# Projections and the first feed-forward matrix as three float32r products of operands split in two, with weights loaded and split per layer, in a new order of work

## The reference, cut to what matters

```
def mha(qx, kx, wq, bq, wk, bk, wv, bv, wo, bo, mask, bias):
    q, k, v = (heads(t @ w + b) for t, w, b in ((qx, wq, bq), (kx, wk, bk), (kx, wv, bv)))
    a = softmax(mask(q @ k.T * scale + bias))
    return merge(a @ v) @ wo + bo
x = layernorm(x + mha(x, x, ...))        # attention 0, windowed
x = layernorm(x + mha(x, ctx, ...))      # attention 1
x = layernorm(x + gelu(x @ w1 + b1) @ w2 + b2)
...
```

## Time and profile before

| | |
|---|---|
| median of 3 runs | 3558.05 us (3555.76 to 3560.11) |
| profiled execution, from first to last instruction | 3565.0 us (no other time of it is given) |
| PE busy | 3446.8 us, 97% |
| DVE busy | 2572.8 us, 72% |
| ACT busy | 1935.0 us, 54% |
| POOL busy | 1143.4 us, 32% |
| granted TensorE clock, mean | 0.992 of 2.4 GHz |

### The profile page before, as it was taken

One profiled execution on the slowest core, in us unless ns is written; L12 is line 12 of the kernel. 1 busy time (PEld: TensorE's weight loads), 2 busy tenths in 40 slices (PEclk: granted clock), 3 DMA queues, 4 the chain that ended last, 5 costly groups with the idle time before them and its releaser, 6 DMA issues.

```text
span 3565.0 us, 53384 instructions
## 1 busy us (share of the span) xinstructions
PE 3446.8 (97%) x18672; PEld 1657.1 (46%) x18932; DVE 2572.8 (72%) x6523; ACT 1935.0 (54%) x2375; POOL 1143.4 (32%) x1049
## 2 busy tenths in 40 slices
PE   8899999999999999999999999999999999999998
PEld 5545544433454554443354455444335445445333
DVE  5766887756886588766778668777577956976667
ACT  2454565555555456555555545555564654655555
POOL 4322432222532242222253223222235322322222
PEclk9999999999999999999999999999999999999999
DMA  6311321223321231122332122112133312211211
GB/s 213 123 46 55 118 67 54 86 60 93 103 78 43 81 114 46 54 87 60 93 123 74 47 93 82 47 53 87 60 109 110 96 54 81 66 46 63 75 54 55
DMA packets 284317, 280.64 MB, mean 79 GB/s; under 512 B 49858, under 2 KB 275266, under 8 KB 280066
## 3 DMA queue, kind: packets, MB, share of 16 engines
q1 hardware_dynamic: 258324, 274.84, 24.0%
q10 hardware_dynamic: 25728, 2.36, 0.6%
HBM read 195.84 MB, written 81.26 MB: 78 GB/s over the span
## 4 chain that ended last, share of the span: by engine, by line
PE 83%; DVE 11%; issue 2%; ACT 2%; DMA 1%; SPq 1%; POOL 0%; another core or an unknown queue 0%; ACTq 0%; DVEq 0%
PE pv L718 14%; PE st L693 14%; PE mx L670 13%; PE mx L768 10%; PE mx L645 10%; PE st L731 9%; DVE row_max L911 5%; PE mx L742 4%; PE st L654 4%; PE mx L765 2%; PE st L778 2%; DVE mx L914 2%; ACT probs L829 1%; DVE turned L934 1%; DMA rows_of_max_dram<-max_rows 1%
## 5 line engine op out<-in xcount | busy, mean ns | idle before, releaser
L829 ACT ACTIVATE probs<-st 128x1024 f32<-128x1024 f32 (+1 forms) x1344 | 1266.6, 977 | 696.4 <-PE st L693 419.1
L911 DVE TENSOR_REDUCE row_max<-mx 128x1 bf16<-128x512 f32 x2048 | 1283.8, 684 | 216.3 <-PE mx L670 121.0
L1021 POOL TENSOR_TENSOR qm<-q_high,own_rows 128x512 bf16<-128x512 bf16 x768 | 797.3, 1044 | 1583.5 <-PE mx L670 1183.6
L670 PE MATMUL mx<-k_high,qm 128*128 128x512 bf16 (+4 forms) x2812 | 815.2, 342 | 44.7 <-DVE row_max L911 18.2
L693 PE MATMUL st<-q_packed,k_packed 97*128 97x512 bf16 (+2 forms) x3072 | 816.0, 346 | 27.3 <-DMA q_packed<-q_parts_dram 9.9
L718 PE MATMUL pv<-probs,va 128*32 128x512 f32 (+2 forms) x6144 | 701.8, 532 | 12.0 <-ACT probs L829 7.1
L670 PEld LDWEIGHTS mx<-k_high,qm 128*128 128x128 bf16 x3072 | 284.3, 98 | 604.0 <-DVE row_max L911 211.1
L914 DVE CUSTOM_DVE_ANT_0 mx<-mx,tab 128x192 f32<-128x192 f32 (+4 forms) x1024 | 400.9, 444 | 132.4 <-PE mx L670 118.7
L693 PEld LDWEIGHTS st<-q_packed,k_packed 97*128 97x128 bf16 (+1 forms) x3072 | 279.6, 98 | 435.0 <-ACT probs L829 149.8
L731 PE MATMUL st<-xT,w1s 128*128 128x512 f32 x768 | 342.9, 592 | 0.0
L957 DVE TENSOR_TENSOR y<-mx,row 128x256 f32<-128x256 f32 x224 | 94.8, 423 | 299.9 <-PE mx L768 297.2
(11 more groups left out here) (88 smaller groups left out, 3141.5 us busy)
## 6 DMA issues: line engine op xcount, KB each, us to landing
k_packed<-k_parts_dram SPq DMA_DIRECT2D x576, 128.0 KB, 2.7
q_packed<-q_parts_dram SPq DMA_DIRECT2D x576, 128.0 KB, 2.7
q_parts_dram<-q_low SPq DMA_DIRECT2D x96, 256.0 KB, 2.2
k_parts_dram<-k_low SPq DMA_DIRECT2D x96, 256.0 KB, 2.5
q_parts_dram<-q_high SPq DMA_DIRECT2D x48, 256.0 KB, 2.1
k_parts_dram<-k_high SPq DMA_DIRECT2D x48, 256.0 KB, 2.3
w1s<-w_dram SPq DMA_DIRECT2D x12, 1024.0 KB, 5.1
w2s<-w_dram SPq DMA_DIRECT2D x12, 1024.0 KB, 7.6
```

Of the source, the lines that this page charges most:

```text
L670: mm = pe.matmul(bank[:, 0:k1 - k0], qm[:, h % RING, i * P:(i + 1) * P], high["k"][s][:, t, k0:k1], start=True, stop=True)
L829: act.activation(dst[:, :, 0:w], held["scores", b, a, n, e][:, :, 0:w], ACT.Exp, scale=ATT_SCALE[a]) \
L911: ins = dve.tensor_reduce(top, scores, AX_X, ALU.max, negate=True)
L1021: pool.tensor_tensor(qm[:, h % RING], high["q"][s][:, h // HT], own_rows[:, h % HT:h % HT + 1].to_broadcast([P, TOK]), ALU.mult) \
```

## The change

The products of `project`, `project_v`, `hidden` and of the attentions' outputs are each written as three float32r matmuls. Both operands are cut in two: a high part, which ScalarE writes by a copy into a float32r tile, and a low part, which GpSimd computes as the original minus the high part. The product is then high x high + high x low + low x high. The second feed-forward matrix, scores, maxima, values, transpositions and folds stay as they were.

- Activations: new tiles `xh`/`xl` (state), `ch`/`cl` (context, and the input of a new pair) and `oh`/`ol` (attention output). A stage `low` cuts one half of an input, 128 x 2 x 256 or 128 x 512.
- Weights: `sq` now holds one layer's four squares in two parts. Stages `fetch` and `split` load one matrix (256 KB) into the single buffer `raw_w` and cut it, once for each pair of sequences; `fetch_w` and `split_w` do the same with quarters of `w1`. A fetch waits for GpSimd's part of the cut before. The folds' results go to DRAM and are fetched from there.
- Order: a sixth list of stages holds the weights' stages, and all strings of `MERGE` are new.

```
+def weight_stages(j):
+    b, a = LOOPS[j]
+    nb, na = (b // SLOTS * SLOTS + (SLOTS if a == 5 else 0), (a + 1) % 6)
+    if b % SLOTS:
+        yield from list(squares_of(nb, na, "qkv" if own(na) else "kvq"))[1:]
+    else:
+        yield from squares_of(b, a, "o")
+        if not j:
+            yield from w1_of(0, 0)
+        elif a in (2, 4, 5):
+            yield from w1_of(b + SLOTS * (a == 5), {2: 1, 4: 2, 5: 0}[a])
+        yield "fetch", nb, na, "q" if own(na) else "k"
...
 MERGE = {
...
-    "01": "011110111011101112301210111130111011101121122121011212103111011022111011211110011120010222222222"
-           "0002222020000222002002202220220200202220002222222",
...
+    "01": "101111102101104121101110101111130114212122432101110420110122101111022101431201201110112001221131"
+           "201222221022220220201230220202202202002022222020002022022020",
...
-        sq = sb("sq", [P, len(SQ), KT, D])
+        sq = sb("sq", [P, 4, 2, KT, D])
         w1s = sb("w1s", [P, KT, FF])
+        w1l = sb("w1l", [P, KT, FF])
+        raw_w = sb("raw_w", [P, KT, D])
...
+        def product(pe, bank, parts, start, stop):
+            for n, (stationary, moving) in enumerate(parts):
+                mm = pe.matmul(bank, stationary.bitcast(F32R), moving.bitcast(F32R), start=start and n == 0,
+                               stop=stop and n == len(parts) - 1)
+            return mm
...
+                elif kind == "fetch" and b < B:
+                    a, m = stage[2:]
+                    free_raw(stage)
+                    of = fold_dram[FOLDS.index(f"{m}{a}")] if f"{m}{a}" in FOLDS else square(f"{m}{a}")
+                    sp.dma_start(raw_w[:].rearrange("p k n -> p (k n)"), of).then_inc(raw_in, 16)
...
                     for t in range(KT):
                         bank = held["proj", b, a, m, t] = mx_bank()
-                        for j in range(KT):
-                            mm = pe.matmul(bank, sqw(f"{m}{a}")[:, j, t * P:(t + 1) * P], src[:, j, :],
-                                           start=(j == 0), stop=(j == KT - 1))
-                        mm.then_inc(*mx_filled.mark(("proj", b, a, m, t)))
+                        at = slice(t * P, (t + 1) * P)
+                        product(pe, bank, [(weight(m, w)[:, j, at], xs[:, j, :]) for j in range(KT) for w in range(2)], True, False)
+                        if t == 0:
+                            pe.wait_ge(*pool_step.past(("low", b, tag, 1)))
+                        product(pe, bank, [(weight(m, 0)[:, j, at], ls[:, j, :]) for j in range(KT)], False, True) \
+                            .then_inc(*mx_filled.mark(("proj", b, a, m, t)))
...
+                elif kind == "low":
+                    tag, p = stage[2:]
+                    highs, k, at = lows[low_place(b, tag)][0], *piece(tag, p)
+                    if p == 0:
+                        read = LAST_READ[b, tag]
+                        if read:
+                            act.wait_ge(*(mx_filled if read[0] == "mx" else st_filled).past(read[1]))
+                    act.wait_ge(*raw_made(b, tag, p))
+                    act.activation(highs[:, k, at].bitcast(F32R), raw(b, tag)[:, k, at], ACT.Identity) \
+                        .then_inc(*act_step.mark(("high", b, tag, p)))
...
+                elif kind == "split" and b < B:
+                    a, m = stage[2:]
+                    pool.wait_ge(*act_step.past(stage))
+                    pool.tensor_tensor(weight(m, 1).bitcast(F32R), raw_square(b, a, m), weight(m, 0), ALU.subtract) \
+                        .then_inc(*pool_step.mark(stage))
...
+                elif kind == "low":
+                    tag, p = stage[2:]
+                    (highs, rests), (k, at) = lows[low_place(b, tag)], piece(tag, p)
+                    pool.wait_ge(*act_step.past(("high", b, tag, p)))
+                    pool.tensor_tensor(rests[:, k, at].bitcast(F32R), raw(b, tag)[:, k, at], highs[:, k, at], ALU.subtract) \
+                        .then_inc(*pool_step.mark(stage))
```

405 lines of the change are left out of this document (280 added, 125 removed).

## The result

The changed kernel takes **3479.18 us** (median of four runs, 3478.05 to 3480.68), beside 3556.91 us (3555.37 to 3560.11) for the kernel before on the same chip: a ratio of 0.9778, 95% interval 0.9766 to 0.979. That is 78 us less. The forecast was 182 us less, 3375, and 3479 lies just above the upper end of the range, 3475.

A forecast was written before the change was run, and what follows sets the result against it. TensorE's queue was taken to set the time, with VectorE close behind in light stretches. From 3565 us, -192 for the pace, +7 and +2 for the ends gave 3382, scaled to a median of about 3375; range 3310 to 3475.

The forecast's parts named there:

- the two ends: Start and end of the kernel: 7 us later through the first projections, 2 us more at the last attention's output.
- I take the lower bound: 0.66 and 0.33 us per product. That saves ... 230 us.: Replaced products on TensorE: float32r at bf16's pace, 0.22 us for 512 columns and 0.11 for 256, saves 230 us of queue.
- I believe 60% of it there ... and 95% in the heavy ones.: Share of saved queue seen as time: 60% in light stretches (no feed-forward), 95% in heavy ones (the others); 192 us.
- Neither becomes the bound. The cover is what these engines have free.: 448 splits on ScalarE (65% of the span) and GpSimd (half) stay hidden in those engines' free time.
- The cover ahead of the first feed-forward: Element 0, last turn of x to first w1s product: 3.0 us of copies and splits hidden behind 4.9 + 0.9 us.
- Ends: +7 at the start.: First projection waits for low parts of wq and x; first complete product at about 17 us, three projections about 7 later.
- VectorE's share up to 76%: Sign of being right: VectorE's busy share of the span, 72% before, rises to 76%.
- light stretches that do not shrink: Sign of being wrong: stretches of a round without feed-forward do not get shorter at all.
- half pace: Rival, 10%: float32r streams at the pace of today's float32 halves, 495 us more, about 4050 us.
- the weight loads: Rival, 10%: three weight loads per product bind the 256-column products, 106 us of queue less, about 3465 us.
- The cover fails: Rival, 12%: splits late in ScalarE's or GpSimd's queue cost each of 48 stretches 2 us, about 3470 us.
- VectorE binds: Rival, 8%, said VectorE doesn't bind: maxima spread well, nearly all 230 us seen, about 3335 us or less.

The follow-up runs named there:

- run 2: Kernel before in its own order, each replaced product issued as three float32r matmuls of one constant rounded tile, no splits: 3408.57 us, ratio 0.9574.
- run 5: Changed kernel with GpSimd's 448 subtractions and ScalarE's 448 copies both cut to 16 columns: 3423.72 us, ratio 0.9616.
- run 4: Changed kernel with only GpSimd's 448 subtractions cut to 16 of 512 columns: 3422.1 us, ratio 0.9608.
- run 12: Changed kernel with each of the 448 subtractions issued as two of 256 columns, the 96 old 1024-column ones as two of 512: 3444.37 us, ratio 0.9682.
- run 7: Kernel before plus 432 GpSimd subtractions of 128x512 whose result nobody reads: 3585.24 us, ratio 1.0072.
- run 16: Kernel before in the new order, each replaced product as three float32r matmuls of constant tiles, no splits or fetches: 3412.52 us, ratio 0.9585.

## Why the prediction was wrong

From run 2 on there is a chain of medians: 3559 before, 3409 with the pace alone (-150), 3413 with the new order (+4), 3424 with fetches and short splits (+11), 3479 with GpSimd's full subtractions (+55 to 57). The forecast had -192 for the pace, nothing for the next three, and +9 for the two ends: 42 + 4 + 11 + 55 - 9 = 103 of the 104 us between 3375 and 3479.

- **"I take the lower bound: 0.66 and 0.33 us per product. That saves ... 230 us."** The mechanism was right, the size wrong. A float32r instruction goes at 0.233 us for 512 columns, a tenth slower than bf16's 0.213, and three of them make a product 0.70 us: 182 us of queue. This term alone is 48 us of queue, 40 of time. The 0.22 and 0.11 us were a lower bound taken as the value.
- **"I believe 60% of it there ... and 95% in the heavy ones."** Right. With 182 us a light stretch has 2.5 us to lose, a heavy one 5.1: 0.6 x 15.2 + 0.95 x 30.4 = 38 us a round, 152 in all, and run 2 gave 150. By kind it was 10.3 of 15.2 and 30.5 of 30.4 in the round looked at (four such rounds would be 163; the traced execution of before was 7 us longer than its median). This holds for the pace alone; in the changed kernel the held operations eat most of it.
- **"Neither becomes the bound. The cover is what these engines have free."** This step failed, and cost the most. The busy shares were right (ScalarE 62%, GpSimd 49%), ScalarE's copies are hidden (run 5), and TensorE hardly waits for a low part. But a GpSimd instruction isn't free for VectorE: while it runs, scale and `normal` stand still. The 448 subtractions cost 57 us (run 4), a term that the sum put at nothing. TensorE's waits for y and for row maxima, both made by VectorE, shrank by 39.5 us when they were cut. How much of the 57 goes this way is bounded and not fixed: halving the instructions' length, with more GpSimd work, gave 35 us back (run 12, in which the old 1024-column ones are halved too), and the same kind of instruction with no reader cost 26 in the old kernel (run 7). The rest may be low parts that come late or a shift of the whole schedule; no run separates it.
- **The cover ahead of the first feed-forward**, 4.9 + 0.9 us against 3.0: right. TensorE's idle time ahead of all 384 matmuls of x's low parts on w1 sums to 0.3 us.
- **Ends: +7 at the start.** The first projection starts at 17.31 us, as worked out ("about 17"), but the first attention ends at 98.4 us in place of 105.7. The relief for the resident squares' 2.5 MB, to which nothing was given back, is one candidate; no run separates it.
- **The order's own cost** was no term of the sum. It is 17 us in float32 and 4 at the new pace.
- **"VectorE's share up to 76%"** came out, 77%, by luck: the forecast got it from a shorter span, and the trace from 96 us more of VectorE's time in a longer one. Of the signs of being wrong that it named, none but "light stretches that do not shrink" appeared, and that in two of six: the failure wasn't among them.

Of the rivals, half pace fell (0.233 us), and so did the weight loads: a float32r load stands for 188 to 195 ns, yet 256-column instructions follow every 0.118 us. "The cover fails" has a price of 3470, near the result, by luck: its splits late in ScalarE's queue cost nothing when cut, and TensorE's products wait 6.8 us in all for GpSimd. The maxima's weight loads do wait for masks, 29.3 us where before has 2.9, but that comes with the order (37.9 in run 16) and costs little there. VectorE binds, more than forecast.
## What to carry to other kernels

Before work is put on GpSimd because it is idle, list VectorE's operations that read and write SBUF and stand on the critical path, and look how long they are when a GpSimd instruction runs beside them; a mean over the group hides it. What counts is whether TensorE waits behind them: 59 us more of held time went with 4 us in one pair of runs (2 and 16), 41 us with 57 in another (4 and the changed kernel). If the work has to go there, shorter instructions can help, up to a point: halved subtractions won 35 us, and halving the masks and quartering the 1024-column ones too lost 21 of them again. And cost a new instruction type with a pace between its bounds, not at the lower one, when the whole gain is a small difference of two large products.
